# One kernel step re-cut: a leaking unit folded into a matrix product, shorter inverse roots, a score looked up by its known value, and two score products that nobody reads

## What is computed

```python
# layer 0, mixer: patches of 96 channels x 9 positions, 512 vectors w_mask
y = einsum('ncij,vc->nvij', patches, w_mask) / (x_norm * w_norm)
idx = argmax(y.reshape(NL, -1), axis=1)       # best vector and best position
max_ch, max_col = idx // 9, idx % 9
sim_map_max = y[max_ch]                        # its 9 similarities
integrate = max_act * max_sim + w_mask[max_ch] * (1 - max_sim)
inp = concatenate([integrate, sim_map_max], axis=1)          # 96 + 9
h = leaky_relu(inp @ w_i1.T + b_i1, 0.2)                     # 288
vcs = tanh(h @ w_i2.T + b_i2)                                # 96
h1 = relu(vcs @ w_l1.T + b_l1)
out = (h1 @ w_l2.T + b_l2) then w_conv
# FFN of both layers: q_mul rounds to 2 mantissa bits
hid = relu(q_acc(q_mul(x) @ q_mul(W1).T) + q_mul(b1)); y = q_mul(hid) @ q_mul(W2).T + ...
# layer 1, mixer: x / (2 + 1e-4 * box5x5(sum_c x^2)) ** 0.75, then LayerNorm
```

## Time and profile before

| | |
|---|---|
| median of 3 runs | 3665.52 us (3658.46 to 3670.87) |
| the profiled execution | 3659.15 us, span 3657.4 us |
| busy share of the span | DVE 85%, PE 83%, ACT 79%, POOL 70% |
| mean granted TensorE clock | 0.945 of the upper level |

### The profile page before, as it was taken

How to read it: one execution, slowest core, us unless ns; L and a number is a source line. 1 busy time by engine, 2 the same in 40 slices (tenths; PEclk the granted TensorE clock), 3 DMA queues, 4 the chain that set the end, 5 groups by cost and what they waited for, 6 DMA issues and landing times. The chain is left out here.

```text
span 3657.4 us, 63346 instructions
## 1 busy us (share of the span) xinstructions
PE 3038.1 (83%) x17928; PEld 1674.1 (46%) x17928; DVE 3093.2 (85%) x11127; ACT 2890.6 (79%) x7558; POOL 2569.9 (70%) x3993
## 2 busy tenths in 40 slices
PE   5887888888888888888888888888888888888755
PEld 2444454444445444444444444444444444444332
DVE  6788989889888998889889888889998888999631
ACT  0444888878788887878878788888888888888877
POOL 2455677767777777777767777776777777777753
PEclk9999999999999999999999999999999999999855
DMA  3111111111111121111111111121211111111000
GB/s 84 45 37 45 46 60 54 60 50 56 58 55 60 50 65 50 57 58 55 60 50 57 58 55 55 55 65 50 60 55 56 59 50 61 54 59 46 23 30 34
DMA packets 64515, 195.70 MB, mean 54 GB/s; under 512 B 11392, under 2 KB 14633, under 8 KB 64169
## 3 DMA queue, kind: packets, MB, share of 16 engines
q1 hardware_dynamic: 53928, 172.76, 14.8%
q0 software_dynamic: 10240, 18.89, 2.1%
HBM read 134.60 MB, written 57.02 MB: 52 GB/s over the span
## 5 line engine op out<-in xcount | busy, mean ns | idle before, releaser
L385 PE MATMUL banks<-wcT,xc 128*128 128x512 f32 x2304 | 1217.4, 631 | 108.8 <-DVE mx L731 104.2
L518 ACT ACTIVATE ffn_hid<-banks 128x384 f16<-128x384 f32 x2304 | 1026.8, 487 | 296.5 <-PE banks L362 273.1
L731 DVE TENSOR_REDUCE mx<-banks 128x1 f32<-128x512 f32 x1152 | 774.7, 683 | 227.9 <-PE banks L385 218.4
L362 PE MATMUL banks<-ffn_xT,w1q 128*128 128x384 bf16 x2304 | 678.1, 348 | 177.4 <-ACT ffn_hid L518 138.3
L994 POOL TENSOR_TENSOR ffn_f<-ffn_y,b2q 128x864 f16<-128x864 f16 x256 | 469.7, 1835 | 375.5 <-DVE nb L717 300.1
L362 PEld LDWEIGHTS banks<-ffn_xT,w1q 128*128 128x128 bf16 x2304 | 228.7, 100 | 790.6 <-ACT ffn_hid L518 588.1
L385 PEld LDWEIGHTS banks<-wcT,xc 128*128 128x128 f32 x2304 | 422.6, 199 | 350.8 <-DVE mx L731 150.8
L817 DVE TENSOR_SCALAR ffn_hid<-ffn_hid,b1q 128x1152 f16<-128x1152 f16 x768 | 420.9, 559 | 126.1 <-ACT ffn_hid L518 126.0
L996 POOL TENSOR_TENSOR x<-x,ffn_f 128x864 f32<-128x864 f32 x256 | 488.3, 1907 | 20.1
L551 ACT ACTIVATE ffn_x<-x,cols 128x96 fp8e5<-128x96 f32 x1152 | 461.4, 456 | 0.0
L551 ACT ACTIVATE ffn_x<-x,nb,roots 128x96 fp8e5<-128x96 f32 x1152 | 424.9, 455 | 0.0
(11 more groups left out here) (147 smaller groups left out, 4474.0 us busy)
## 6 DMA issues: line engine op xcount, KB each, us to landing
xt<-x_tok_in SPq DMA_DIRECT2D x128, 432.0 KB, 3.2
xc<-x_chan_in SPq DMA_DIRECT2D x128, 432.0 KB, 3.6
out_tok<-x SPq DMA_DIRECT2D x128, 432.0 KB, 2.5
win<-x_tok_in,xrow POOLq DMA_INDIRECT x128, 2.6
wrow<-vector_table,vidx POOLq DMA_INDIRECT x128, 2.7
shift<-shift_in SPq DMA_DIRECT2D x1, 960.0 KB, 5.7
vector_table<-wtab SPq DMA_DIRECT2D x1, 384.0 KB, 3.3
w1raw<-w_in SPq DMA_DIRECT2D x1, 288.0 KB, 6.4
```

The source lines that it names most:

```text
L362: last = pe.matmul(bank[:, 0:GW], w1q[:, ffn.layer, c * P:(c + 1) * P], ffn.xT[:, g * GW:(g + 1) * GW], start=True, stop=True)
L385: last = pe.matmul(ps_score[score_bank(j)], xc[p][:, j, :], wcT[:, :], start=True, stop=True)
L518: return nc.scalar.activation(dst, src, ACT.Copy)
L731: nc.vector.tensor_reduce(mx[p][:, j:j + 1], ps_score[score_bank(j)], AX.X, ALU.max).then_inc(score_taken, 1)
```

## The change

- `D1` grows by one: `inp` gets a column of ones, so that the bias `b_i1` comes in through the product `mlp_in`. The leaking unit is written as 0.8 relu(z) + 0.2 z. ACT makes `h` = relu(0.8 z) from PSUM in one instruction over 384 columns; `leaky` on DVE and `z1` go. The 0.2 z part is linear, so it is multiplied out ahead of the loop into `leak` (0.2 times w_i1 with its bias, times w_i2), and `mlp_mid` starts with one more product, `leak` with `inpT`.
- `win_vector` no longer takes a maximum. `select` makes a third accumulated product, of `pick` and `mx`, which is the known best score, into `vtop`; the place of that value is searched in the 512 scores.
- `inverse_root` has eight links for eleven: the guess, then one round of four with a polynomial of second degree, then one round of three with the factor -0.5 moved into the square; the halved copy is gone.
- `pick` compares with the integer index, repeated over the columns; the cast to float (L753) is gone.
- `hidden` does its three ReLUs first and then one rounding over all 3456 columns; `hid_ready` counts once a tile.
- `keep_busy` on PE: two products `xc[p][:, j]` with `wcT` into `ps_b`, that nobody reads, ahead of `mlp_turn` and behind the output units of `tail`, in every step that has `f1` and `f3` and no `lrn`. The output of the kernel is not touched by them, since `mlp_in` overwrites `ps_b`.
- In the set-up: one more weight load (`wi1r`), three more products, one more ACT instruction, a few memsets.

```diff
+ROOT_POLY = np.polynomial.Chebyshev.interpolate(
+    lambda w: w ** -0.5, 2, domain=[0.9324, 1.0691]).convert(kind=np.polynomial.Polynomial).coef
...
-                            pe.wait_ge(ffn.hid_ready, (tile + 1) * HC)
+                            pe.wait_ge(ffn.hid_ready, tile + 1)
...
+            def keep_busy(f1, f3, p):
+
+
+                wait_past(pe, x1_ready, f3)
+                for j in range(2):
+                    pe.matmul(ps_b, xc[p][:, j, :], wcT[:, :], start=True, stop=True)
+
...
                 pe.wait_ge(h_ready, f3 + 1)
+                pe.matmul(ps_a[0:C, 0:P], leak[:, :], inpT[:, :], start=True, stop=False)
                 for c in range(M1):
-                    last = pe.matmul(ps_a[0:C, 0:P], wi2[:, c, :], h[:, c, :], start=(c == 0), stop=(c == M1 - 1))
+                    last = pe.matmul(ps_a[0:C, 0:P], wi2[:, c, :], h[:, c, :], start=False, stop=(c == M1 - 1))
...
                 if k.f3 is not None:
+                    if k.f1 is not None and k.lrn is None:
+                        keep_busy(k.f1, k.f3, k.q)
                     mlp_turn(k.f3)
...
-                    for c in range(M1):
-                        last = nc.scalar.activation(z1[:, c * P:(c + 1) * P], ps_b[0:C, c * P:(c + 1) * P],
-                                                    ACT.Identity, bias=bmlp[:, c:c + 1])
-                    last.then_inc(z1_ready, 1)
+                    nc.scalar.activation(h[:].rearrange("c m p -> c (m p)"), ps_b[0:C, 0:M1 * P], ACT.Relu,
+                                         scale=1.0 - LEAK).then_inc(h_ready, 1)
...
-            def inverse_root(chain, x, y, t, xh):
+            def inverse_root(chain, x, y, t):
...
-                chain.add(nc.vector.tensor_scalar(y.bitcast(i32), x.bitcast(i32), -0.5, ROOT_SEED, ALU.mult, ALU.add),
-                          nc.vector.tensor_scalar(xh, x, -0.5, None, ALU.mult))
-                yield
-                for _ in range(3):
+                stt = nc.vector.scalar_tensor_tensor
+                chain.add(nc.vector.tensor_scalar(y.bitcast(i32), x.bitcast(i32), -0.5, ROOT_SEED, ALU.mult, ALU.add))
+                yield
+                for scale, inner, outer in ((ROOT_POLY[2] ** 0.5, ROOT_POLY[1] / ROOT_POLY[2] ** 0.5, ROOT_POLY[0]),
+                                            (-0.5, None, 1.5)):
                     chain.wait()
-                    chain.add(nc.vector.tensor_tensor(t, y, y, ALU.mult))
+                    chain.add(stt(out=t, in0=y, scalar=float(scale), in1=y, op0=ALU.mult, op1=ALU.mult))
                     yield
                     chain.wait()
-                    chain.add(nc.vector.tensor_tensor(t, t, xh, ALU.mult))
+                    chain.add(nc.vector.tensor_tensor(t, t, x, ALU.mult))
                     yield
+                    if inner is not None:
+                        chain.wait()
+                        chain.add(stt(out=t, in0=t, scalar=float(inner), in1=t, op0=ALU.add, op1=ALU.mult))
+                        yield
                     chain.wait()
-                    chain.add(nc.vector.scalar_tensor_tensor(out=y, in0=t, scalar=1.5, in1=y, op0=ALU.add,
-                                                             op1=ALU.mult))
+                    chain.add(stt(out=y, in0=t, scalar=float(outer), in1=y, op0=ALU.add, op1=ALU.mult))
...
-                f1c.add(nc.vector.tensor_copy(jf[:, :], jidx[:, 0:1]))
-                yield
-                f1c.wait()
-                f1c.add(nc.vector.tensor_scalar(pick[p][:, :], iota[:, :], jf[:, 0:1], None, ALU.is_equal))
+                f1c.add(nc.vector.tensor_tensor(pick[p][:, :], iota[:, :], jidx[:, 0:1].broadcast_to([P, J]),
+                                                ALU.is_equal))
...
+                nc.vector.scalar_tensor_tensor(out=junk[:, 2, :], in0=pick[p][:, :], scalar=1.0, in1=mx[p][:, :],
+                                               op0=ALU.mult, op1=ALU.mult,
+                                               accum_out=vtop[p][:, 0:1]).then_inc(pick_ready, 1)
...
-                f2c.add(nc.vector.max(vtop[:, :], ps_score[0]))
-                next(between, None)
-                f2c.wait()
-                nc.vector.max_index(vidx[:, :], vtop[:, :], ps_score[0]).then_inc(vidx_ready, 1)
+                dve.wait_ge(pick_ready, f2 + 1)
+                nc.vector.max_index(vidx[:, :], vtop[q][:, :], ps_score[0]).then_inc(vidx_ready, 1)
...
-                relu(0)
-                run(between, 1)
-                for c in range(1, HC):
+                for c in range(HC):
                     relu(c)
                     run(between, 1)
-                    round_up(c - 1)
-                    run(between, 1)
-                round_up(HC - 1)
+                dve.wait_ge(ffn.rounded, (tile + 1) * HC)
+                bits = ffn.hid[:, :, :].rearrange("p c n -> p (c n)").bitcast(U16)
+                nc.vector.tensor_scalar(bits, bits, TO_E5M2, TO_E5M2, ALU.add,
+                                        ALU.subtract).then_inc(ffn.hid_ready, 1)
+                run(between, 1)
```

## The result

The changed kernel takes **3621.6 us** (median of 4 runs, 3620.4 to 3623.6); the kernel before, run beside it, 3666.7 (3658.5 to 3670.9). The ratio is 0.988, with a 95% interval of 0.986 to 0.990: 45 us faster, where 15.5 were forecast. The profiled execution took 3623.6 us around a span of 3621.8, 35.6 less than the one of before.

The account below looks back on a forecast made before the run. No engine clearly bounded it: a lap was ACT and PE for 17.6 us, DVE some 5, then PE. Terms of -1.2 us an image gave -17.5, the drain +3, so a median of 3650 us; range 3600 to 3692.

Parts of the forecast that it names:

- the first images: The first image, without layer 1: the same trades with other sizes, put at nothing.
- What the products buy: Two unread products on PE fill the stretch ahead of clock falls outside LRN steps; falls gone, -2.9 us an image.
- Ordinary step: Loop step without the LRN chain: next `vcs` 0.45 us late, from 25.38 to 25.83 us; six an image, +2.7.
- The joined rounding: Three DVE roundings as one after the last ReLU: 0.97 us, bounds 0.93 and 1.11, with 0.5 us of cover.
- The known maximum: DVE's maximum over 512 columns, 0.70 us, goes; no gain on the path, covered by PE and ACT.
- LRN step: Step with the LRN chain: start -0.8 us, end -0.2; PE's wait 1.5 to 2.7 us, clock still falls.
- The drain: End of the run: one rounding of 0.97 us or more for two in 0.82; +0.25 for some eleven tiles, +3.
- From the profiled run to the median: The profiled run lay 6.4 us under the median; this was added to 3644.6, giving about 3651.
- A: Rival, chance 0.09: the products are free, ordinary steps go to 25.0 us; 3575 us.
- B: Rival, chance 0.11: POOL and the ReLUs no longer collide in the LRN step, its clock fall goes; 3612 us.
- C: Rival, chance 0.17: clock falls outside the LRN step stay and steps pay 0.45 us each; 3692 us.
- D: Rival, chance 0.13: joined rounding or integer comparison runs slower; rounding about 3.5 us, over 3830 us; small loss 3663.

Follow-up runs that it names:

- e1: The changed kernel without the two products that nobody reads; 3558.0 us, ratio 0.977.
- c4: The kernel before with the eight-link roots alone, second of three runs, in another session; 3535.0 us, ratio 0.971.
- d0: The kernel before with the eight-link roots alone, third of three runs; 3534.9 us, ratio 0.970.
- b1: The kernel before with the eight-link roots alone, first of three runs; 3701.3 us, ratio 1.008.
- e9: The changed kernel without the two unread products and with the old eleven-link roots in each step; 3631.6 us, ratio 0.997.
- e6: The changed kernel, products kept, with the old eleven-link pixel roots in each step; 3639.6 us, ratio 0.999.
- e2: The changed kernel with one unread product in place of two; 3555.3 us, ratio 0.975.
- b3: The changed kernel without its two products, with three unread products in each LRN step and one a step in the first images; 3542.9 us, ratio 0.966.
- d1: The kernel before with the eight-link roots alone, plus two unread ACT copies ahead of the copy of layer 1's second output unit; 3554.0 us.
- c1: The changed kernel without its two products and with the leaking unit back on DVE; 3551.2 us, ratio 0.975.

## Why the prediction was wrong

The sign was right and most of the walk, the size was not: 15.5 us forecast, 45 measured, 21 beside the session in which before stood at 3642. Two steps failed. In size it is **the first images, a term put at nothing**: -19.3 us, nearly all of the 21 us by which the profiled executions miss the sum (3644.6 said, 3623.6 measured). In mechanism it is **"What the products buy"**: the falls go without the products. Term by term:

- **Ordinary step:** 25.83 said, 25.74 measured. Leak product 0.22 said and measured; PE's two waits for DVE used up by the products, as said. DVE alone was to give 25.0: 24.86 (e1).
- **The joined rounding** lasts 1.05 and is spaced 0.96 (0.97 taken, bounds 0.93 and 1.11) and is free, as said. **The known maximum** is worth nothing in an ordinary step, as said.
- **LRN step:** -1.0 said in all (start -0.8, end -0.2); means 31.85 before, 30.51 after, -1.34. PE's wait there is 2.82 (said 1.5 to 2.7), and the clock still falls. The ReLU that collides there (L834) starts at 543.08 and takes 2.27 until 545.35, while POOL's L993 ends at 545.03: the collision moved from L693 to the ReLU, as said.
- **"What the products buy".** The falls outside the LRN step were taken as a term of their own, -2.9 us an image, that only the products could earn, so that DVE's part appeared as a change of 0.4 a step with the falls left in place. The runs show that either part ends the falls: products alone 0 of 91, all of DVE's part 0 of 91, new roots alone 1 of 91 in c4 and d0 (but 20 in b1), DVE's part with the old roots 8 (e9), none of them 10 to 19. So the term was real and stood in the right sum. But with DVE's part in place the two products earn nothing of it in the 13 images, and cost 0.87 a step. The steady part came to -19.3 for 13 images, where the sum had -15.6: right in the sum, with the credit given to the wrong half.
- **The first images** were put at nothing; they are -19.3 us, the largest single miss. There the steps are 23.65 before and 23.1 after; beside the very first step, where the clock is low for a while in both, five of the first 16 had a fall and none has now. DVE's part gives 11.3 of the 19.3 (389.7 in e1 for 401.0), the products the other 8.0. e6 shows that the roots carry part of that (23.7 again with the old ones), e2 and b3 that a product carries part (23.1 against 24.0). "The same trades with other sizes" was a guess where the trace had 16 steps to walk.
- **The drain:** +3 said for the rest, nothing to be seen: with its share of the steady part the last stretch was to come to +1.1, and is +0.4. Set-up, not in the sum, is +2.6.
- **From the profiled run to the median:** 6.4 us were carried over as a constant. They are not one: before's time depends on how many falls an execution has, and on the session; the changed kernel, with none, lies within 5 us in all its runs. That alone is 8 of the miss, and 25 between sessions.
- **Rivals.** A (the products are free) falls: the second costs in full. B falls: PE's wait in the LRN step is 2.82 and the clock falls there. C falls: no fall is left outside. The Trainium skill's page "TensorE: Matmul & The Clock Gate", section "Why this matters for your kernels", ties drops to long idle gaps; in before the clock fell 15 of 19 times with no single gap of PE over 0.59 us in the half step ahead of it (the other four had one of 0.73 to 1.92), and it stopped falling in e1 with gaps of about 0.4 left. The measurement decides: here gaps far below the page's length go with falls. D falls: the rounding is 1.05, not over 1.2. Its large price, 3.5 us for the rounding, does not follow from its row either: 3456 columns at 0.69 us for 512 are 4.7.

What stays open: why new roots or one product alone suffices to hold the clock; and what makes PE's signal late, often in one session, seldom or never in the others.

## What to carry to other kernels

Before a repair is paid for (here work that nobody reads), make the other half of the change alone and count the event that it is to stop: the shorter chain had already stopped it, and the repair cost 63 us of a gain of 86. An instruction of DVE with two SBUF inputs that becomes ready close to the start of a long POOL instruction is a switch: 0.06 us more or less decided over 1.4 us a step in d0 and d1. Such a kernel needs several sessions before its time is believed. Moving the instruction to ACT brought nothing on the day (c1); that it pays in a session with late signals is likely, but not shown. Walk the first images as a part of their own, and compare a kernel only with runs beside it.

## What was not expected of the hardware

- PE's signal for a finished group of matmuls can come 0.6 to 0.8 us after the recorded end of the last one, mostly at one place of a kernel and in one session: in 94 steps of the new roots alone (0 in its two other profiles), in 105 units of before (0 in its other two). The ordinary steps of before did not become longer by it (25.36); where it led to a held DVE instruction (b1) they were 1.6 us longer.
- A DVE instruction of 0.55 us that came 0.04 us after the start of a POOL instruction of 1.82 took 2.18; coming 0.02 before it, it took 0.55 and POOL's took 2.21 (d1, d0).
- The kernel before moved between 3642 and 3672 us from session to session, the changed one, run in two of them, stood at 3620.8 and 3621.6 beside 3642 and 3667.
- The best time of all, 3535 us, belongs to the smallest edit, the roots alone, and so does the worst, 3701. The fastest version whose leaking unit is not on DVE (b3, 3543) ran in the very session of that 3701.
